# A three-pass graph network: the second edge pass loads edge messages that the first one stored, instead of computing them again

## The chip, the cores and the metric

The kernel runs on one core of one Trainium2 chip. The metric is the device time of one execution in microseconds (us), as the median of three unprofiled runs. The engines are PE (TensorE), DVE (VectorE), ACT (ScalarE), POOL (GpSimd) and SP (SyncE, which here issues DMAs only).

## The reference

The graph has 12,500 nodes of 96 features and 412,500 directed edges, sorted by their target node. Two GINE convolutions are followed by a residual layer norm, and then by a message-passing layer with batch statistics over all edges and nodes:

```python
e = relu(edge_weight @ W_l0 + b_l0) @ W_l1 + b_l1      # (edges, 96), the same e in both convolutions
def gine_conv(x, W1, b1, W2, b2):
    msg = relu(x[src] + e)
    h = x + segment_sum(msg, dst)
    return relu(relu(h @ W1 + b1) @ W2 + b2)
h = relu(gine_conv(relu(gine_conv(x, ...)), ...))
x = layernorm(x + h)
# then: edge_feat = mlp(edge_attr_4), message = mlp([x[src], x[dst], edge_feat]),
# out = layernorm(x + segment_sum(message, dst) + mlp(x)); each mlp normalizes over all its rows
```

## The kernel before

**Work.** Edges are cut into 124 slabs of 26 tiles of 128 edges. A slab is worked on in seven chunks: six of four tiles and one of two. Three passes go over all 868 chunks: `conv0` (first convolution), `conv1` (second convolution, and beside it the edge features of the last layer and their batch statistics, `stats=True`) and `last`. A loop iteration `k` covers four slabs, `Q = 28` chunks, so a pass has 31 iterations. Chunk `q` of iteration `k` has the running number `n = Q*k + q`.

**One chunk of a convolution.** POOL gathers the source nodes' rows with one indirect DMA for each tile (`gather`, L264), 104 for an iteration and 3,224 for a pass, 9,672 in all. PE makes the hidden edge layer (`hidden`, L543, bank `ps_hid`), ACT applies its relu (`relu_hidden`, L556), PE makes the edge message (`pre`, L1309) in one of two banks `ps_pre`. DVE adds the gathered rows in the bank (`add_gathered`, L641). The result is split into three bf16 parts so that a bf16 matmul sums it exactly: ACT takes part one (L582), DVE subtracts it (L589), ACT takes part two (`second_part`, L595), DVE part three (`third_part`, L600). DVE also makes a one-hot matrix of the targets (L1385), and PE sums the chunk into a window of nodes (`segment`, L606, bank `ps_win`). In `conv1` PE also makes the edge features (L549), ACT applies their relu (L562) and DVE takes their statistics (L628).

**Order.** Each engine has its own instruction stream. `staged` writes it: a plan is a list of (lag, stage), and in step `q` every stage does its work for chunk `q - lag`. Semaphores count chunks. A stage waits for the count of what it reads, and for the count that says its buffer is free. `pre` of chunk n waits for part three of chunk n-2, since there are two banks. Node layers of finished nodes are placed beside the chunks from iteration 8 on.

**POOL's waits.** The gathers of chunk n wait until the rows of chunk n-28 have been added (`add`), since the row buffers hold an iteration. Two more waits in `close` tie POOL to PE:

```python
if i == 0:
    sem, count = "seg", Q * k + q - 4 - (6 if opening(k) else 0)
elif i == 2:
    sem, count = "pre", Q * k + q - 1 - (4 if opening(k) else 0)
```

The first gather of a chunk waits until `segment` is four chunks behind at most, the third until `pre` is one behind. In `conv0` these two waits begin with iteration `NEAR = 3`; in the other passes they are there from the start.

Of the kernel before, what the change touches and what calls it, by code (L numbers as in the profile page):

```python
# [18 lines left out]
F32 = mybir.dt.float32  # L19
# [18 lines left out]
Q = V * NC_  # L38
QH = U * NC_
# [68 lines left out]
def staged(eng, iters, width, plan, ahead=None, start=None, side=()):  # L108

    parts = V // U
    half = width // parts

    def beside(k, late, q):
        h, at = q // half, q % half
        for place, stage in side:
            if late > 0 and place == at:
                stage((k - start) * parts + h)
            if (late > 1 or (late and h)) and place == at + half:  # L120
                stage((k - start) * parts + h - 1)
# [12 lines left out]
    for place, stage in side:  # L134
        if place >= half and start < iters:
            stage((iters - start) * parts - 1)
    for q in range(max(lag for lag, _ in plan)):
        for lag, stage in plan:
            if q < lag:
                stage(iters - 1, width + q - lag)  # L140
# [8 lines left out]
def gnn_kernel(nc, a, out):  # L149
# [22 lines left out]
    with ctx:  # L172
# [70 lines left out]
        w_hid0_rows = nc.dram_tensor("w_hid0_rows", (KW, C), BF16, kind="Internal").ap()  # L243
        near = nc.dram_tensor("near", (S, T * P), BF16, kind="Internal").ap()
# [164 lines left out]
        def edge_pass(name, table, y=None, split_edges=False, stats=False, last=False):  # L409
# [8 lines left out]
            with ExitStack() as st:  # L418
# [18 lines left out]
                hid = [sb(f"{name}_hid{i}", [P, CH * P], F32, st) for i in range(2)]  # L437
# [35 lines left out]
                if not last:  # L473
                    z = sb(f"{name}_z", [C1, STEP], F32, st)
                    END = STEPS - inner_steps(N, NPAD, S)
                    assert END % 2 == 0 and 2 * STEP <= 512
# [25 lines left out]
                turned = [x[:, 512 - W:512] for x in ps["win"]]  # L502
                s = Sems(st, name)
# [4 lines left out]
                NEAR = 3  # L508

# [8 lines left out]
                def load_rows(sp, r, slab):  # L518
# [3 lines left out]
                    for i in range(3):  # L522
                        sp.dma_start(row[r][AT + i * n:AT + (i + 1) * n, :], src[:, at]).then_inc(s[f"row{r}"], 16)
# [22 lines left out]
                def features(pe, r, q, b, n, free):  # L546
                    t0, nt = CHUNKS[q % NC_]
                    need(pe, s["rf"], n)
                    pe.matmul(ps["feat"][0][0:C, 0:nt * P], w_hid1[0:KE, 0:C], srow[r][:, t0 * P:(t0 + nt) * P],  # L549
                              start=True, stop=True).then_inc(s["f"], 1)  # L550
# [7 lines left out]
                def relu_features(act, q, b, n, free):  # L558
                    nt = CHUNKS[q % NC_][1]
                    act.wait_ge(s["f"], n + 1)  # L560
                    need(act, s["bn"], free)
                    act.activation(feat[b][:, 0:nt * P], ps["feat"][0][0:C, 0:nt * P], ACT.Relu).then_inc(s["rf"], 1)  # L562
# [74 lines left out]
                def add_gathered(v, j, q, b, n):  # L637
                    t0, nt = CHUNKS[q % NC_]
                    v.wait_ge(s["pre"], n + 1)
# [325 lines left out]
                def tensor_end(pe):  # L965
                    for r in range(U):
                        pe.wait_ge(s[f"win{r}"], ITERS * PAIRS)
                    pe.wait_ge(s["step"], STEPS - END + 1)
                    for w in ENDS:
# [38 lines left out]
                def scalar_end(act):  # L1008
# [3 lines left out]
                    if split_edges:  # L1012
# [3 lines left out]
                        for w in ENDS:  # L1016
                            act.activation(sums[0:C, end_at(w):end_at(w) + 2 * STEP], one[w][0:C, :], ACT.Relu,
                                           bias=b_conv[l][1][:]).then_inc(s["e_sums"], 1)
                        return
# [130 lines left out]
                def sync_windows(sp):  # L1150
# [29 lines left out]
                    def slab_rows(k, j):  # L1180
                        r = j % U
                        free("hid", k, j)
                        if stats:
                            free("f", k, j)
                        load_rows(sp, r, k * V + j)
# [67 lines left out]
                def gpsimd_windows(gp):  # L1253
                    def close(k, q, i):
# [4 lines left out]
                        elif i == 2:  # L1259
# [28 lines left out]
                def tensor_windows(pe):  # L1288
                    def hidden_rows(k, q):
                        j, c, _, _ = chunk(q)  # L1290
                        r = j % U
                        if c == 0:
                            pe.wait_ge(s[f"row{r}"], ROWS * (turn(k, j) + 1))
                        hidden(pe, r, q, Q * k + q)
                        if stats:
                            if c == 0:
                                pe.wait_ge(s[f"srow{r}"], 48 * (turn(k, j) + 1))
                            features(pe, r, q, q % 2, Q * k + q, left(k, q))

# [34 lines left out]
                    staged(pe, ITERS, Q, [(0, hidden_rows), (1, pre), (4, turn_window), (3, segment)],  # L1334
                           start=START, side=([] if last else [(4, summed)]) + node_stages(pe))

                def scalar_windows(act):
                    plan = [(0, lambda k, q: relu_hidden(act, q, q % 2, Q * k + q, left(k, q)))]
                    if stats:
                        plan += [(0, lambda k, q: relu_features(act, q, q % 2, Q * k + q, left(k, q)))]  # L1340
# [4 lines left out]
                    plan += [(2, lambda k, q: second_part(act, q, q % 2, Q * k + q)), (1, message)]  # L1345
                    if last:
                        plan += [(1, lambda k, q: square_message(act, q, q % 2, Q * k + q, left(k, q)))]
                    staged(act, ITERS, Q, plan, ahead=(lambda k: copy_piece(act, k)) if split_edges else None,
                           start=START, side=node_stages(act))

                def vector_windows(v):
# [38 lines left out]
                    def add_rows(k, q):  # L1390
# [5 lines left out]
                        add_gathered(v, j, q, q % 2, Q * k + q)  # L1396
# [110 lines left out]
                def vector_general(v):  # L1507
# [3 lines left out]
                    def body(k):  # L1511
# [6 lines left out]
                        for c, (t0, nt) in enumerate(CHUNKS):  # L1518
# [17 lines left out]
                            add_gathered(v, 0, c, 0, n)  # L1536
# [390 lines left out]
```

## Time and profile before

| What | Value |
|---|---|
| Median of three unprofiled runs | 12209.71 us (12207.5 to 12210.12) |
| Span of the profiled execution | 14691.4 us |
| PE busy in that span | 9543.3 us, 65% |
| DVE busy | 7533.7 us, 51% |
| ACT busy | 4925.7 us, 34% |
| POOL busy | 9148.4 us, 62% |
| DMA | 647.55 MB, mean 44 GB/s |

The profiled execution's own time is its span, from the first to the last instruction of the program. It is 20% longer than the unprofiled median. Busy shares are over the whole span; the three passes take about a third of it each (`conv0` to 4,859 us, `conv1` from 4,880 to 9,729 us, `last` from 9,770 us), and a short stretch of final layers ends it. Times of POOL's gathers are those of writing the descriptors; the data moves afterwards.

### The profile page before, as it was taken

Reading aid. Unit: us, or ns where it says so; the run is one execution under the profiler, and the core shown is the slowest. Engines: PE = TensorE matmul, PEld = TensorE weight load, DVE = VectorE, ACT = ScalarE, POOL = GpSimd, SP = SyncE. Lnnn points to the kernel's source line nnn. Section 1 sums busy time; section 2 is a strip of 40 time slices with the busy share of each in tenths; the row PEclk is TensorE's granted clock in tenths of the full one; section 3 lists DMA queues with packets and bytes.
Section 4 is the critical chain, followed back from the end, with each engine's and each line's share of the span. In section 5 each row is a group of like instructions: output and inputs, shape, how many; then the busy total and the mean of one; then the engine's idle time right before and its main releaser. Section 6 shows DMA issues by size and latency. Waiting matters only on the chain. (4 is left out here: it accounts for less than half of the span.)

```text
span 14691.4 us, 164775 instructions
## 1 busy us (share of the span) xinstructions
PE 9543.3 (65%) x34164; PEld 6790.2 (46%) x34164; DVE 7533.7 (51%) x15604; ACT 4925.7 (34%) x11020; POOL 9148.4 (62%) x9725
## 2 busy tenths in 40 slices
PE   3666666666666677777777777766555555555556
PEld 2544444444444444455555555544444444444444
DVE  3433434334333444455555555556666666666666
ACT  2322222222222333333333333333333333333333
POOL 6466666666666566666666666656666666666665
PEclk9999999999999655555555555555555555555555
DMA  3111111111111211122222222211122222212122
GB/s 80 32 40 40 40 41 40 41 40 40 41 40 40 54 42 43 43 47 45 46 46 46 47 46 45 47 43 41 42 45 43 44 43 44 44 44 44 43 44 47
DMA packets 580837, 647.55 MB, mean 44 GB/s; under 512 B 411208, under 2 KB 411689, under 8 KB 579722
## 3 DMA queue, kind: packets, MB, share of 16 engines
q0 software_dynamic: 309504, 476.02, 15.5%
q1 hardware_dynamic: 219142, 139.69, 3.9%
q10 hardware_dynamic: 51712, 27.54, 0.7%
q14 instruction: 432, 3.54, 0.1%
q8 instruction: 47, 0.77, 0.0%
HBM read 604.68 MB, written 39.43 MB: 44 GB/s over the span
## 5 line engine op out<-in xcount | busy, mean ns | idle before, releaser
L1309 PE MATMUL ps_pre<-w_e,conv_hid 97*128 97x96 f32 x12896 | 3268.4, 433 | 2144.1 <-DVE conv_part L600 1554.4
L1309 PEld LDWEIGHTS ps_pre<-w_e,conv_hid 97*128 97x128 f32 x12896 | 2873.9, 326 | 2886.6 <-issue 2393.8
L1309 PE MATMUL ps_pre<-last_w_q,last_hid 128*128 128x96 f32 x6448 | 1627.8, 432 | 1540.8 <-issue 935.3
L1309 PEld LDWEIGHTS ps_pre<-last_w_q,last_hid 128*128 128x128 f32 x6448 | 1440.1, 327 | 1928.3 <-issue 1605.6
L264 POOL DMA_INDIRECT early_got<-in_x_rows,early_idx x1612 | 1524.3, 946 | 960.5 <-issue 439.0
L264 POOL DMA_INDIRECT early_got<-h_rows,early_idx x1612 | 1520.8, 943 | 944.2 <-issue 478.3
L264 POOL DMA_INDIRECT early_got<-p_rows,early_idx x1612 | 1520.4, 943 | 926.6 <-issue 463.3
L264 POOL DMA_INDIRECT last_got<-p_rows,early_idx x1612 | 1520.8, 943 | 905.0 <-issue 430.5
L264 POOL DMA_INDIRECT conv_got<-h_rows,early_idx x1612 | 1520.8, 943 | 884.0 <-issue 435.6
L264 POOL DMA_INDIRECT conv_got<-in_x_rows,early_idx x1612 | 1520.7, 943 | 853.1 <-issue 447.1
L582 ACT ACTIVATE conv_part<-ps_pre 128x384 bf16<-128x384 f32 x1736 | 816.0, 470 | 3676.9 <-DVE ps_pre L641 2405.4
L606 PE MATMUL ps_win<-conv_part,conv_hot 128*112 128x288 bf16 x6448 | 1904.0, 445 | 0.6 <-DVE conv_part L600 0.5
L556 ACT ACTIVATE conv_hid<-ps_hid 96x512 f32<-96x512 f32 x1736 | 972.8, 560 | 2311.5 <-remote 1488.0
L641 DVE TENSOR_TENSOR ps_pre<-ps_pre,early_got 128x384 f32<-128x384 f32 x1302 | 697.2, 536 | 1982.9 <-remote 697.7
L1385 DVE TENSOR_TENSOR conv_hot<-ps_own,rel 128x448 bf16<-128x448 f32 x1736 | 1016.2, 585 | 1082.3 <-remote 359.4
L543 PE MATMUL ps_hid<-conv_row,w_hid 12*96 12x512 bf16 x1736 | 1084.7, 625 | 545.4 <-issue 343.6
L606 PEld LDWEIGHTS ps_win<-conv_part,conv_hot 128*112 128x112 bf16 x6448 | 1290.7, 214 | 78.0 <-DVE conv_part L600 2.5
L641 DVE TENSOR_TENSOR ps_pre<-ps_pre,conv_got 128x384 f32<-128x384 f32 x868 | 466.5, 537 | 1469.3 <-remote 715.4
L628 DVE BATCH_NORM_STATS2 conv_parts<-conv_feat 96x6 f32<-96x512 f32 x868 | 563.8, 649 | 782.4 <-issue 460.0
L606 PE MATMUL ps_win<-last_part,last_hot 128*112 128x291 bf16 x3224 | 964.0, 450 | 0.6 <-DVE last_part L600 0.5
L595 ACT CAST conv_part<-ps_pre 128x384 bf16<-128x384 f32 x1736 | 787.7, 454 | 469.8 <-DVE ps_pre L589 269.7
L600 DVE TENSOR_TENSOR conv_part<-ps_pre,conv_part 128x384 bf16<-128x384 f32 x1736 | 905.0, 521 | 77.7 <-issue 65.4
(255 smaller groups left out, 10572.7 us busy)
## 6 DMA issues: line engine op xcount, KB each, us to landing
conv_row<-ea_parts SPq DMA_DIRECT2D x372, 84.5 KB
last_row<-ea_parts SPq DMA_DIRECT2D x372, 84.5 KB
early_got<-in_x_rows,early_idx POOLq DMA_INDIRECT x1612
conv_got<-in_x_rows,early_idx POOLq DMA_INDIRECT x1612
early_got<-h_rows,early_idx POOLq DMA_INDIRECT x1612
conv_got<-h_rows,early_idx POOLq DMA_INDIRECT x1612
early_got<-p_rows,early_idx POOLq DMA_INDIRECT x1612
last_got<-p_rows,early_idx POOLq DMA_INDIRECT x1612
```

The lines of the kernel that those rows point to most:

```text
L264: gp.indirect_dma_start(to[:, t * C:(t + 1) * C], None, table, bass.IndirectOffsetOnAxis(index[:, t:t + 1], 0)).then_inc(sem, 16)
L543: pe.matmul(ps["hid"][0][0:HC, 0:nt * P], w_hid[:], row[r][AT:AT + K, t0 * P:(t0 + nt) * P], start=True, stop=True).then_inc(s["hid"], 1)
L556: act.activation(hid[b][0:C, 0:nt * P], ps["hid"][0][0:C, 0:nt * P], ACT.Relu).then_inc(s["rhid"], 1)
L582: act.activation(part_of(q, 0, nt)[:, :, 0:C], m3, ACT.Relu).then_inc(s["part0"], 1)
L595: act.copy(part_of(q, 1, nt)[:, :, 0:C], tiles_of(ps["pre"][b], nt, C)).then_inc(s["part1"], 1)
L600: v.tensor_tensor(part_of(q, 2, nt)[:, :, 0:C], tiles_of(ps["pre"][b], nt, C), part_of(q, 1, nt)[:, :, 0:C], ALU.subtract).then_inc(s["par ...
L606: return pe.matmul(bank[0:W, 0:3 * M].rearrange("p (i c) -> p i c", i=3), hot_b[:, t * W:(t + 1) * W], parts, start=start, stop=stop)
L628: v.bn_stats(parts[:, c * 6:(c + 1) * 6], feat[b][:, 0:nt * P]).then_inc(s["bn"], 1)
L641: v.tensor_tensor(at, at, got[j][:, t0 * C:(t0 + nt) * C], ALU.add).then_inc(s["add"], 1)
L1309: mm = pe.matmul(ps["pre"][q % 2][:, t * C:(t + 1) * C], hid[q % 2][0:P if last else C1, t * P:(t + 1) * P], w_q[j % U][:, c * C:(c + 1) * ...
L1385: v.tensor_tensor(hot[q % 2][:, 0:nt * W].rearrange("p (t w) -> p t w", w=W), iota[:, 0:W].unsqueeze(1).to_broadcast([P, nt, W]), rel[:, b ...
```

## The change

`e` is the same in both convolutions, so `conv0` keeps it. There ACT copies the message from the PSUM bank to one of four SBUF ring buffers before the rows are added (`keep_messages`), and one step later issues a DMA that stores the chunk in a DRAM tensor `e_rows` (`store_messages`, 128 partitions of 1,536 bytes for a four-tile chunk, 192 KB). DVE's `add_gathered` waits for the copy (`ecp`) in place of PE's `pre`.

In `conv1` the hidden layer and `pre` are gone from PE, `relu_hidden` from ACT, the loads of the edge weights from SP and the wait on `pre` from POOL. ACT issues a load of the chunk three of its steps ahead (`load_messages`) and copies it into the bank (`bring_messages`). ACT's plan is shifted by two steps against the others for that, and the edge features get a second PSUM bank.

```diff
-                for i in range(3):
+                for i in range(3 if weights else 0):
...
+                def keep_messages(act, k, q, b, n):
+                    nt, slot = CHUNKS[q % NC_][1], q % ER
+                    act.wait_ge(s["pre"], n + 1)
+                    need(act, s[f"est{slot}"], 16 * (USES * k + q // ER))
+                    act.copy(e_ring[slot][:, 0:nt * C], ps["pre"][b][:, 0:nt * C]).then_inc(s["ecp"], 1)
...
+                def store_messages(act, k, q, n):
+                    j, _, t0, nt = chunk(q)
+                    slot = q % ER
+                    act.wait_ge(s["ecp"], n + 1)
+                    act.nop(nofuse=True)
+                    act.dma_start(e_rows[bass.ds(k * V + j, 1), :, t0 * C:(t0 + nt) * C].rearrange("s p c -> (s p) c"),
+                                  e_ring[slot][:, 0:nt * C]).then_inc(s[f"est{slot}"], 16)
...
+                def load_messages(act, k, q, n):
+                    need(act, s["ecp"], n + 1 - ER)
+                    act.dma_start(e_ring[slot][:, 0:nt * C], e_rows[...]).then_inc(s[f"eld{slot}"], 16)
+                def bring_messages(act, k, q, b, n, free):
+                    act.wait_ge(s[f"eld{slot}"], 16 * (USES * k + q // ER + 1))
+                    need(act, s["part2"], free)
+                    act.copy(ps["pre"][b][:, 0:nt * C], e_ring[slot][:, 0:nt * C]).then_inc(s["ecp"], 1)
...
-                    v.wait_ge(s["pre"], n + 1)
+                    v.wait_ge(ready, n + 1)
...
-                        elif i == 2:
+                        elif i == 2 and not stats:
...
-                    staged(pe, ITERS, Q, [(0, hidden_rows), (1, pre), (4, turn_window), (3, segment)],
+                    staged(pe, ITERS, Q, [(0, hidden_rows), *([] if stats else [(1, pre)]), (4, turn_window), (3, segment)],
...
+                    elif stats:
+                        plan = [(0, lambda k, q: load_messages(act, k, q, Q * k + q)),
+                                (SHIFT + 1, lambda k, q: bring_messages(act, k, q, q % 2, Q * k + q, left(k, q))),
+                                (SHIFT, lambda k, q: relu_features(act, q, q % 2, Q * k + q, left(k, q))),
+                                (SHIFT + 2, second), (SHIFT + 1, message)]
+                    else:
+                        plan = [(0, hidden_part), (2, second),
+                                (1, lambda k, q: keep_messages(act, k, q, q % 2, Q * k + q)), (1, message),
+                                (2, lambda k, q: store_messages(act, k, q, Q * k + q))]
```

Line numbers in the rows below this point are each kernel's own. ACT in the middle of `conv0`, two steps before:

```order
L556 ACTIVATE conv0_hid1<-ps1_hid0 96x512
L595 CAST conv0_part3<-ps1_pre1 128x4x96
L582 ACTIVATE conv0_part0<-ps1_pre0 128x4x96
L554 REGISTER_ALU
L556 ACTIVATE conv0_hid0<-ps1_hid0 96x512
L595 CAST conv0_part0<-ps1_pre0 128x4x96
L582 ACTIVATE conv0_part1<-ps1_pre1 128x4x96
```

ACT at the same place now (L570 is `relu_hidden`, L642 `second_part`, L583 the new copy, L629 part one, L591 the store with the empty instruction ahead of it):

```order
L570 ACTIVATE conv0_hid1<-ps1_hid0 96x512
L642 CAST conv0_part1<-ps1_pre1 128x4x96
L583 COPY conv0_e_ring2<-ps1_pre0 128x384
L629 ACTIVATE conv0_part2<-ps1_pre0 128x4x96
L591 ISA
L591 DMA e_rows<-conv0_e_ring1 128x384
L568 REGISTER_ALU
L570 ACTIVATE conv0_hid0<-ps1_hid0 96x512
L642 CAST conv0_part2<-ps1_pre0 128x4x96
L583 COPY conv0_e_ring3<-ps1_pre1 128x384
L629 ACTIVATE conv0_part3<-ps1_pre1 128x4x96
```

Each step has gained a copy between part two of one chunk and part one of the next, and a store at its end.

PE in the middle of `conv1` before (L543 hidden layer, L549 features, L1309 `pre`, L606 `segment`):

```order
L543 MATMUL ps2_hid0<-conv1_row1,w_hid0_64 96x512
L549 MATMUL ps2_feat0<-conv1_row1,w_hid1 96x512
L1309 MATMUL ps2_pre0<-w_e0,conv1_hid0 128x96 x4
L606 MATMUL ps2_win1<-conv1_part2,conv1_hot0 112x288 x4
L543 MATMUL ps2_hid0<-conv1_row1,w_hid0_64 96x512
```

PE there now (L563 is the features' matmul, L653 `segment`):

```order
L563 MATMUL ps2_hid0<-conv1_row1,w_hid1 96x512
L653 MATMUL ps2_win1<-conv1_part2,conv1_hot0 112x288 x4
L563 MATMUL ps2_feat0<-conv1_row1,w_hid1 96x512
L653 MATMUL ps2_win1<-conv1_part3,conv1_hot1 112x288 x4
L563 MATMUL ps2_hid0<-conv1_row1,w_hid1 96x256
```

The hidden layer and the four `pre` matmuls of a chunk are gone, and the features alternate between two banks.

ACT in the middle of `conv1` now (L600 load, L609 copy into the bank, L576 relu of the features); before, the step held L556, L562, L595 and L582:

```order
L600 ISA
L600 DMA conv1_e_all<-e_rows 128x384
L609 COPY ps2_pre0<-conv1_e_all 128x384
L574 REGISTER_ALU
L576 ACTIVATE conv1_feat1<-ps2_hid0 96x512
L642 CAST conv1_part1<-ps2_pre1 128x4x96
L629 ACTIVATE conv1_part2<-ps2_pre0 128x4x96
```

One activation has gone and one copy has come, and the load is issued at the head of the step.

## Rows read from the trace of the kernel before

**Rows 1.** The page's head: span, busy time of each engine and instructions.

```profile
span 14691.4 us, 164775 instructions
PE 9543.3 (65%) x34164; PEld 6790.2 (46%) x34164; DVE 7533.7 (51%) x15604; ACT 4925.7 (34%) x11020; POOL 9148.4 (62%) x9725
```

**Rows 2.** Timeline of POOL around conv0's end: start, duration, idle before and its releaser.

```profile
4836.65 0.94 POOL L264 DMA_INDIRECT conv_got<-in_x_rows,early_idx  x1 [2.87 <-remote]
...
4850.38 0.95 POOL L264 DMA_INDIRECT conv_got<-in_x_rows,early_idx  x1 [0.30 <-issue]
4854.37 0.94 POOL L264 DMA_INDIRECT conv_got<-in_x_rows,early_idx  x1 [3.04 <-remote]
...
4858.11 0.94 POOL L264 DMA_INDIRECT conv_got<-in_x_rows,early_idx  x1 [0.30 <-issue]
4879.71 0.94 POOL L264 DMA_INDIRECT early_got<-h_rows,early_idx  x1 [20.65 <-issue]
```

**Rows 3.** Timeline of POOL: first gather, end of conv1, start of last, last gather.

```profile
2.76 1.14 POOL L264 DMA_INDIRECT early_got<-in_x_rows,early_idx  x1 [2.33 <-DMA early_idx<-in_src_t]
...
9727.86 0.94 POOL L264 DMA_INDIRECT conv_got<-h_rows,early_idx  x1 [0.30 <-issue]
...
9770.50 0.95 POOL L264 DMA_INDIRECT early_got<-p_rows,early_idx  x1 [23.62 <-issue]
...
14618.69 0.95 POOL L264 DMA_INDIRECT last_got<-p_rows,early_idx  x1 [0.30 <-issue]
```

**Rows 4.** Gathers (L264), conv1 and last: window, length, busy (count), clock, DMA share, GB/s.

```profile
5000.00:9700.00 4700.00, 2944.48 (x3122) 0.50 0.20 45
9800.00:14600.00 4800.00, 3007.23 (x3189) 0.50 0.20 43
```

**Rows 5.** Timeline of POOL in conv0, around the start of iteration 3.

```profile
458.34 0.94 POOL L264 DMA_INDIRECT conv_got<-in_x_rows,early_idx  x1 [0.30 <-issue]
547.10 0.94 POOL L264 DMA_INDIRECT early_got<-in_x_rows,early_idx  x1 [87.81 <-PE ps_win L606]
```

**Rows 6.** Windows there: PE, PEld, DVE, ACT, POOL busy, clock, DMA; then L641 alone.

```profile
461.30:558.70 97.40, 91.45 (x340) 68.24 (x341) 60.70 (x125) 41.47 (x85) 7.78 (x9) 1.00 0.06 13
461.30:558.70 97.40, 15.07 (x28) 1.00 0.06 13
```

**Rows 7.** Timeline of all engines in that stretch, one chunk of conv0.

```profile
485.84 2.02 PE L1309 MATMUL ps_pre<-w_e,conv_hid 97*128 97x96 f32 x8
486.60 0.48 ACT L595 CAST conv_part<-ps_pre 128x384 bf16<-128x384 f32 x1
487.90 0.57 DVE L641 TENSOR_TENSOR ps_pre<-ps_pre,early_got 128x384 f32<-128x384 f32 x1 [1.33 <-PE ps_pre L1309]
488.38 0.55 DVE L600 TENSOR_TENSOR conv_part<-ps_pre,conv_part 128x384 bf16<-128x384 f32 x1
488.50 0.49 ACT L582 ACTIVATE conv_part<-ps_pre 128x384 bf16<-128x384 f32 x1 [1.42 <-DVE ps_pre L641]
489.07 0.50 PE L1309 MATMUL ps_pre<-w_e,conv_hid 97*128 97x96 f32 x1
```

**Rows 8.** Timeline: conv0's first add of gathered rows.

```profile
120.93 0.57 DVE L641 TENSOR_TENSOR ps_pre<-ps_pre,early_got 128x384 f32<-128x384 f32 x1 [1.30 <-PE ps_pre L1309]
```

**Rows 9.** DMAs: an issue by ACT (timeline); two 192 KB stores with their landing.

```profile
7007.28 0.38 ACTq L776 DMA_DIRECT2D nf_rows<-nf  x1
h_rows<-conv_got SPq DMA_DIRECT2D x2, 192.0 KB, 2.2
```

**Rows 10.** The two largest waits of POOL on PE in conv1: us, times, longest.

```profile
POOL early_got L264 <- PE ps_pre L1309: 95.2, 55, 3.1
POOL early_got L264 <- PE ps_win L606: 60.2, 28, 19.1
```

**Rows 11.** Timeline of the first microseconds: a gather and a DVE cast.

```profile
15.97 1.99 POOL L264 DMA_INDIRECT early_got<-in_x_rows,early_idx  x1 [0.30 <-issue]
15.98 1.85 DVE L363 CAST rel<-dst_i 128x3224 f32<-128x3224 int32 x1 [3.64 <-DMA dst_i<-in_dst_t]
```

More of the change, by code:

```diff
@@ L38 @@
 Q = V * NC_
+ER = 4
+USES = Q // ER
 QH = U * NC_
@@ L133, in staged @@
     phases(eng, iters, iters if start is None else start, body)
[L134 to L137, printed above, removed]
+    rest = [(place - half, stage) for place, stage in side if place >= half and start < iters]
+    for q in range(max([lag for lag, _ in plan] + [place + 1 for place, _ in rest])):
+        for place, stage in rest:
+            if place == q:
+                stage((iters - start) * parts - 1)
         for lag, stage in plan:
@@ L436, in edge_pass @@
                 row = [sb(f"{name}_row{r}", [AT + K, T * P], BF16, st) for r in range(U)]
-                hid = [sb(f"{name}_hid{i}", [P, CH * P], F32, st) for i in range(2)]
+                if last:
+                    e_ring = None
+                elif stats:
+                    e_all = sb(f"{name}_e_all", [P, ER * CH * C], F32, st)
+                    e_ring = [e_all[:, i * CH * C:(i + 1) * CH * C] for i in range(ER)]
+                else:
+                    e_ring = [sb(f"{name}_e_ring{i}", [P, CH * C], F32, st) for i in range(ER)]
+                hid = ([e_all[:, i * CH * P:(i + 1) * CH * P] for i in range(2)] if stats else
+                       [sb(f"{name}_hid{i}", [P, CH * P], F32, st) for i in range(2)])
                 msg = [sb(f"{name}_msg{i}", [P, CH * C], F32, st) for i in range(2)] if last else None
@@ L502, in edge_pass @@
                 turned = [x[:, 512 - W:512] for x in ps["win"]]
+                feat_banks = [ps["feat"][0], ps["hid"][0]] if stats else None
                 s = Sems(st, name)
@@ L508, in edge_pass @@
                 NEAR = 3
+                SHIFT = 2
                 def left(k, q):
@@ L547, in features @@
                     t0, nt = CHUNKS[q % NC_]
-                    need(pe, s["rf"], n)
-                    pe.matmul(ps["feat"][0][0:C, 0:nt * P], w_hid1[0:KE, 0:C], srow[r][:, t0 * P:(t0 + nt) * P],
+                    need(pe, s["rf"], free)
+                    pe.matmul(feat_banks[b][0:C, 0:nt * P], w_hid1[0:KE, 0:C], srow[r][:, t0 * P:(t0 + nt) * P],
                               start=True, stop=True).then_inc(s["f"], 1)
@@ L1018, in scalar_end @@
                                            bias=b_conv[l][1][:]).then_inc(s["e_sums"], 1)
+                        for slot in range(ER):
+                            act.wait_ge(s[f"est{slot}"], 16 * USES * ITERS)
                         return
@@ L1181, in slab_rows @@
                         r = j % U
[L1182 to L1185, printed above, removed]
+                        free("f" if stats else "hid", k, j)
+                        load_rows(sp, r, k * V + j, weights=not stats)
                         if last:
@@ L1292, in hidden_rows @@
                         if c == 0:
-                            pe.wait_ge(s[f"row{r}"], ROWS * (turn(k, j) + 1))
-                        hidden(pe, r, q, Q * k + q)
+                            pe.wait_ge(s[f"srow{r}" if stats else f"row{r}"], (48 if stats else ROWS) * (turn(k, j) + 1))
                         if stats:
-                            if c == 0:
-                                pe.wait_ge(s[f"srow{r}"], 48 * (turn(k, j) + 1))
                             features(pe, r, q, q % 2, Q * k + q, left(k, q))
+                        else:
+                            hidden(pe, r, q, Q * k + q)
                     def pre(k, q):
@@ L1395, in add_rows @@
                                 v.wait_ge(s[f"got{j}{g}"], 16 * (t1 - t0) * (k + 1))
-                        add_gathered(v, j, q, q % 2, Q * k + q)
+                        add_gathered(v, j, q, q % 2, Q * k + q, s["pre" if last else "ecp"])
                     def add_constants(k, q):
@@ L1535, in body @@
                                 v.wait_ge(s["qadd"], 2 * n + 2)
-                            add_gathered(v, 0, c, 0, n)
+                            add_gathered(v, 0, c, 0, n, s["pre"])
                             subtract_first(v, c, 0, n)
```

31 lines of the change are left out of this document (21 added, 10 removed).

## The prediction

> **What bounds the kernel now.** I read the page's head first [rows 1]: PE 65%, POOL 62%, DVE 51%, ACT 34%. No engine is full, so the head doesn't name the bound. The timeline of POOL does. Between two waits, twelve gathers of `conv0` start from 4836.65 to 4850.38 us [rows 2], that is 13.73 / 11 = 1.248 us from one start to the next, of which 0.94 is the gather and 0.30 the issue of the next. Multiply it out: 9,672 gathers x 1.248 = 12,070.7 us. Outside that train lie the start, 2.76; the turn from `conv0` to `conv1`, 4879.71 - 4858.11 - 1.25 = 20.4 [rows 2]; the turn to `last`, 9770.50 - 9727.86 - 1.25 = 41.4; and what follows the last gather's slot, 14691.4 - 14618.69 - 1.25 = 71.5 [rows 3]. Together 136.0, the sum 12,206.7. The unprofiled median is 12,209.7. So the unprofiled kernel is POOL issuing gathers without a stop, with 3 us left for real waits; the rounding of the two rows (0.001 us a gather) makes that 3 +- 10. If a slot were only the mean gather, 2944.48 / 3122 = 0.943 [rows 4], and 0.30, the sum would be 12,158 and waits could hold at most 51 us.
>
> The profiled execution lasted 14,691.4 us [rows 1], 2,485 us more than this sum. POOL's timeline shows where: waits of some 3 us put down to "remote", one 4850.38 to 4854.37, the last 4836.65 [rows 2], about 18 us apart, that nothing in the program ends. Both later passes pay the same for them, 4700 / 3122 = 1.505 and 4800 / 3189 = 1.505 us a gather [rows 4], though their layers on the other engines differ. I take them for an effect of the recording. They are not in the median, so my sum is made against the 12,206.7, that is the profiled time without them, which stands 0.02% below the median; differences go on the median as they are. The profiled span after the change can't be compared with 14,691.4 to better than these waits repeat.
>
> The consequence: work taken from PE, ACT or DVE is worth only as much as POOL waits for it, and work added costs only as much as it makes POOL wait.
>
> **The one place where POOL waits for real: `conv0`, iteration 3.** POOL runs three iterations ahead without a bond to PE, and the first gather of iteration 3 waits until `segment` is at chunk 80. In the profile that is 87.81 us, ended by PE [rows 5]. Unprofiled, POOL is there at 2.76 + 312 x 1.248 = 392.1 us. The first add is at 120.93 [rows 8]. In this stretch, with POOL out of the way, 28 chunks took 97.40 us, or 3.48 each, with PE busy for 91.45 of them, 94% [rows 6]. So chunk 80 is summed at 120.9 + 81 x 3.48 + 1.2 for its `segment` = 404.0, and POOL waits 12 us, at the edge of the 3 +- 10 that the sum leaves. From there POOL needs 4.99 us for a four-tile chunk and PE 3.48, and the wait doesn't come back.
>
> **What `conv0` gains in work.** ACT's copy, priced by the cast of the same 128x384 from the bank, 0.48 [rows 7], plus a hand-over between engines: part one starts 0.03 after the add's end (488.50 - 487.90 - 0.57), so 0.52. It lies between `pre` and the add. Follow the loop: `pre` begins at 485.84, the add at 487.90 (2.06), DVE's third part of the chunk before at 488.38 (0.48), and that frees the bank for the `pre` of the next chunk at 489.07 (0.69) [rows 7]. The loop is 3.23, under the 3.48 that PE needs. With the copy it is 3.75, and DVE's order, add before third part, keeps it in a line. PE's chunk of 3.48 is no longer the longer one: +0.27 a chunk. Up to chunk 80 that is 81 x 0.27 = **+22 us**, and POOL's wait grows from 12 to 34. Whether ACT is free when `pre` ends: part two ends at 486.60 + 0.48 = 487.08, 0.8 before [rows 7]. The store's issue, 0.38 [rows 9], and an empty instruction stand behind part one, so the next relu starts about 0.3 late and the margin is still 0.5. Bounds: nothing, if the compute is over 34 us earlier at chunk 80 than I have it; and with nothing hidden, 0.52 + 0.43 for the store, 0.95 x 81 = +77. In the rest of the pass the loop of 3.75 stays under POOL's 4.99, 1.2 us to spare a chunk, and costs nothing; if POOL were not the bound there it would be +0.27 x 787 = +212, but the sum above excludes it. The ring has four buffers: a store has two steps, 7 us at the least, to land, and a store of 192 KB landed in 2.2 us [rows 9]. Nothing.
>
> **What `conv1` loses and gains.** On PE the hidden matmul and the eight `pre` instructions of a chunk, 2.02 us [rows 7], go. ACT trades an activation for a copy and an issue, about equal. POOL's waits on PE there are the largest candidates, 95.2 us in 55 waits of at most 3.1, and 60.2 in 28 waits with one of 19.1 [rows 10]. Waits of 3.1 at most are as long as the recording's own, and the sum of the median has no room for 155 us. I take 0, between 0 and -13 (the 3 + 10). The load is issued three ACT steps ahead, at least 11 us against a landing of 2.2, hidden. At the pass's start the first load and copy take the place of the hidden layer and `pre`; the first gathers land in the meantime. The two ends of the pass I put at +-1.
>
> **Transfers.** 868 chunks, 158.5 MB, are stored in one pass and loaded in the next, in 4,024 us of unprofiled pass 39 GB/s, over the 45 that flow now at a DMA share of 0.20 [rows 4]. A doubled share leaves the engines 60% idle, and POOL waits for a gather's descriptors, never for its landing, since an add has an iteration of slack. The gathers' own duration decides: 0.943 in `conv1` and in `last` alike [rows 4], whatever else flows. It was longer in one place only, 1.99 us beside DVE's cast of 128x3224 in SBUF, 15.97 against 15.98 us [rows 11]. The copies added here are ACT's. By the Trainium skill, "DMA: Bandwidth & Descriptors", SWDGE vs HWDGE vs iDMA, GpSimd writes its descriptors to rings in SBUF, a DVE in its two-port mode locks it out of there, and DMAs issued by ACT or SP are immune to that; by that rule the added transfers cost POOL nothing, and the trace agrees where it has anything to show, the long gather beside the cast.
>
> Sum: 0 at the start, +22 at iteration 3, 0 in the steady state, 0 in `conv1`, 0 in `last`: 12,209.7 + 22 = **12,232 us**.
>
> **Rivals.** *A. Nothing measurable* (24%): the change works, PE's load in `conv1` falls, and the compute of the opening is early enough, or ACT's copy hidden well enough, that POOL's wait at iteration 3 hardly grows. For it: the 3 us that the sum leaves are less than my wait of 12. Against: the wait's releaser is PE in the trace, and the loop has no slack. 12,195 to 12,220.
>
> *B. Faster* (12%): the slot is 1.243 and not 1.248, waits hold 51 us, and 12 of them are iteration 3's. The other 39 then sit in POOL's waits on `pre` and `segment` in `conv1` [rows 10] and vanish with the work: 12,209.7 - 39 + 0 to 10 = 12,171 to 12,185. Against it: over eleven gathers in a row the slot is 1.248, and ACT's chain in `conv1` isn't shorter.
>
> *C. Clearly slower* (18%): the added transfers lengthen the gathers themselves. A tenth of a microsecond on one gather of each of the 1,736 chunks of the two convolutions is +174: 12,383; a gather in fifty at 1.99 in place of 0.94, 129 x 1.05, +135. It passes my forecast's upper side from 0.03 us a chunk on. The mildest form, or a store issue that falls ahead of the copy in the opening, ends at 12,260 to 12,300. Against: the constant 0.943. The Trainium skill, in the section Issuing engines are not separate DMA queues of the same page, says that all DMAs run on the same 16 engines and interleave. By that rule gathers would land later. The rows can show a share of 0.20 only, and no run here shows one of 0.4 yet.
>
> **How the numbers follow.** A measurement of this kernel can tell about 0.2%, 24.4 us, from no change: below 12,185.3 or above 12,234.1. My forecast, a growth of POOL's wait by 10 to 50 us (12,215 to 12,260), has 46%; its point lies so near the bound that I split it 25 within, 21 above. A's 24% are all within. Of B's 12%, 11 are faster. Of C's 18%, all slower. That gives 0.11, 0.50, 0.39. The range of 12,180 to 12,300 leaves out the faster half of B and all of C but its mild form, near 2 in 10; the forecast's own is 12,215 to 12,260.
>
> **What the profile after would show.** Right: L641's adds in the stretch where POOL waits at iteration 3 some 3.75 us apart in place of 3.48, and that wait longer; gathers still 0.943; no wait of POOL on `pre` in `conv1`; PE's busy time at least 1,600 us less (868 chunks at 2.02, one in seven of them half as long); the same gaps at the turns; 317 MB more traffic. Wrong: adds still 3.48 apart (A), gathers longer than 0.943 (C), or gathers closer than 1.248 in a row (B). A turn from `conv0` to `conv1` longer than 20.4 by over 5 us would be something I haven't priced, as would a wait of POOL on `add` in steady `conv0`.

## The result and the profile after

The changed kernel takes **12,293.7 us** (median of 4 runs, 12,288.8 to 12,295.6) against 12,209.9 before (4 runs, 12,207.5 to 12,211.4): ratio 1.0068, 95% interval 1.0054 to 1.0083. It is slower by 84 us. My range of 12,180 to 12,300 holds it, at its very end; it lies outside the 12,215 to 12,260 of the forecast itself, whose point, 12,232, had a quarter of the loss.

The page's head of the changed kernel:

```profile
span 12291.5 us, 156248 instructions
PE 7643.8 (62%) x26848; PEld 5238.2 (43%) x26848; DVE 7456.9 (61%) x15604; ACT 5238.6 (43%) x11888; POOL 9156.0 (74%) x9725
```

The span is 2 us under the unprofiled median. The waits of 3 us that fill the trace of before [rows 2] are gone, and this was not the change's doing: a second trace of the kernel before, taken with the first experiments, is free of them too. It is the one to compare with:

```profile
span 12212.2 us, 164775 instructions
PE 9514.6 (78%) x34164; PEld 6795.0 (56%) x34164; DVE 7482.9 (61%) x15604; ACT 4878.6 (40%) x11020; POOL 9153.9 (75%) x9725
```

The spans differ by 79.3 us. PE has lost 1,871 us of work, ACT has gained 360, and POOL's own time is the same. Where the 79 us lie is read from POOL. The start of iteration 3, in the changed kernel:

```profile
396.51 0.94 POOL L268 DMA_INDIRECT conv_got<-in_x_rows,early_idx  x1 [0.30 <-issue]
427.05 0.94 POOL L268 DMA_INDIRECT early_got<-in_x_rows,early_idx  x1 [29.59 <-PE ps_win L653]
```

and in the second trace of before:

```profile
396.64 0.94 POOL L264 DMA_INDIRECT conv_got<-in_x_rows,early_idx  x1 [0.30 <-issue]
398.46 0.94 POOL L264 DMA_INDIRECT early_got<-in_x_rows,early_idx  x1 [0.88 <-PE ps_win L606]
```

POOL arrives at the same moment in both and now waits 29 us longer. That is the wait of [rows 5]. A second one follows six gathers on. The waits of POOL from 440 to 4,000 us (us in all, times, longest), changed kernel first:

```profile
POOL early_got L268 <- PE ps_pre L1357: 75.4, 81, 5.4
POOL conv_got L268 <- PE ps_pre L1357: 34.1, 112, 0.3
```

and before:

```profile
POOL conv_got L264 <- PE ps_pre L1309: 29.3, 96, 0.3
POOL early_got L264 <- PE ps_pre L1309: 23.5, 77, 0.3
```

A wait of 0.3 is only the issue of the next gather, named after the semaphore that it reads. Longer ones exist in the changed kernel alone, and all of them are at one place: gather 6 of an iteration, the third of its chunk 1, which waits for `pre`. I worked the following out from the gathers' start times, less 1.249 us each:

| Waits of POOL in `conv0`, us | before | after |
|---|---|---|
| opening, before iteration 3 | 5.4 | 5.4 |
| iteration 3, its first gather | 0.6 | 29.3 |
| iteration 3, gather 6 | 1.4 | 5.1 |
| gather 6 of iterations 4 to 30 | 0.0 | 45.5 (25 waits of 1.6 to 2.1) |

The difference is 78.0 of the 79.3. `conv1` and `last` are nearly alike: from first to last gather 4,027.1 and 4,025.4 us after, 4,024.2 and 4,025.3 before.

**What gather 6 waits for.** ACT at the start of iteration 18 (timeline, changed kernel):

```profile
2400.98 0.49 ACT L629 ACTIVATE conv_part<-ps_pre 128x384 bf16<-128x384 f32 x1 [1.90 <-DVE ps_pre L688]
2401.15 0.34 ACTq L591 DMA_DIRECT2D e_rows<-conv_e_ring  x1
2404.79 0.51 ACT L1286 COPY ps_e<-conv_e_f 128x416 f32<-128x416 f32 x1 [3.32 <-issue]
```

The last instruction of iteration 17 is the store's issue; the first of iteration 18 is the copy of a piece of edge attributes. Between them ACT stands, for nothing that the profile names ("issue"). DVE waits behind it, then has five instructions on that piece, and only then its third part:

```profile
2405.43 0.59 DVE L1295 CAST conv_e_p<-ps_e 128x416 bf16<-128x416 f32 x1 [4.48 <-ACT ps_e L1286]
...
2408.45 0.55 DVE L647 TENSOR_TENSOR conv_part<-ps_pre,conv_part 128x384 bf16<-128x384 f32 x1
```

PE's `pre` of chunk 27 needs that bank, and POOL that `pre`:

```profile
2409.05 0.74 PE L1357 MATMUL ps_pre<-w_e,conv_hid 97*128 97x96 f32 x2 [8.94 <-DVE conv_part L647]
2411.00 0.94 POOL L268 DMA_INDIRECT early_got<-in_x_rows,early_idx  x1 [2.31 <-PE ps_pre L1357]
```

At the same place before, ACT goes on at once and DVE waits 1.12:

```profile
2346.78 0.49 ACT L582 ACTIVATE conv_part<-ps_pre 128x384 bf16<-128x384 f32 x1 [3.01 <-DVE ps_pre L641]
2347.24 0.51 ACT L1237 COPY ps_e<-conv_e_f 128x416 f32<-128x416 f32 x1
2347.87 0.59 DVE L1246 CAST conv_e_p<-ps_e 128x416 bf16<-128x416 f32 x1 [1.12 <-ACT ps_e L1237]
```

The record of ACT's sequencer, which the timeline leaves out, says what ACT does in the gap (start, duration, operation; after, then before):

```
2401.59 0.04 L93 COMPARE_BRANCH        2346.85 0.04 L91 COMPARE_BRANCH
2404.65 0.05 L93 FUSED_REGOPS          2347.09 0.05 L91 FUSED_REGOPS
```

It is the branch back to the loop's first instruction. I call the time from the branch's end to that instruction the turn: 2.9 us in the median of 21 after, 0.19 before. An iteration of that loop holds 365 of ACT's instructions after and 197 before. So two theories stood against each other: the loop's turn (theory 1), and the copy that now lies between `pre` and the add (theory 2). A third is the traffic of the stores (theory 3).

### The profile page after: what moved, and what is told of

The parts are those of the page before. It is cut to its first block and busy times, and to the rows that moved or that the text cites. A ratio compares the mean times of both kernels' runs of the same rounds, so it can differ in the third digit from the quotient of the medians.

```text
span 12291.5 us, 156248 instructions
## 1 busy us (share of the span) xinstructions
PE 7643.8 (62%) x26848; PEld 5238.2 (43%) x26848; DVE 7456.9 (61%) x15604; ACT 5238.6 (43%) x11888; POOL 9156.0 (74%) x9725
## 5 line engine op out<-in xcount | busy, mean ns | idle before, releaser
L653 PE MATMUL ps_win<-conv_part,conv_hot 128*112 128x288 bf16 x6448 | 1937.9, 451 | 1811.8 <-DVE conv_part L647 1811.6
L1357 PE MATMUL ps_pre<-w_e,conv_hid 97*128 97x96 f32 x6448 | 1630.6, 433 | 937.8 <-DVE conv_part L647 928.2
L653 PEld LDWEIGHTS ps_win<-conv_part,conv_hot 128*112 128x112 bf16 x6448 | 1207.0, 209 | 2234.7 <-DVE conv_part L647 2140.3
L629 ACT ACTIVATE conv_part<-ps_pre 128x384 bf16<-128x384 f32 x1736 | 815.8, 470 | 2800.7 <-DVE ps_pre L688 2763.8
L1357 PEld LDWEIGHTS ps_pre<-w_e,conv_hid 97*128 97x128 f32 x6448 | 1440.7, 328 | 1318.8 <-issue 1041.7
L653 PE MATMUL ps_win<-last_part,last_hot 128*112 128x291 bf16 x3224 | 964.4, 450 | 1.2 <-DVE last_part L647 1.1
L642 ACT CAST last_part<-ps_pre 128x384 bf16<-128x384 f32 x868 | 397.9, 458 | 1310.7 <-DVE ps_pre L636 1308.5
L642 ACT CAST conv_part<-ps_pre 128x384 bf16<-128x384 f32 x1736 | 785.7, 453 | 342.4 <-DVE ps_pre L636 327.8
L636 DVE SCALAR_TENSOR_TENSOR ps_pre<-ps_pre,conv_part 128x384 f32<-128x384 f32 x1736 | 912.4, 526 | 0.1
```

Source lines behind the costliest of these rows:

```text
L629: act.activation(part_of(q, 0, nt)[:, :, 0:C], m3, ACT.Relu).then_inc(s["part0"], 1)
L636: v.scalar_tensor_tensor(out=m3, in0=m3, scalar=0.0, in1=part_of(q, 0, nt)[:, :, 0:C], op0=ALU.max, op1=ALU.subtract).then_inc(s["rem"], 1)
L642: act.copy(part_of(q, 1, nt)[:, :, 0:C], tiles_of(ps["pre"][b], nt, C)).then_inc(s["part1"], 1)
L653: return pe.matmul(bank[0:W, 0:3 * M].rearrange("p (i c) -> p i c", i=3), hot_b[:, t * W:(t + 1) * W], parts, start=start, stop=stop)
L1357: mm = pe.matmul(ps["pre"][q % 2][:, t * C:(t + 1) * C], hid[q % 2][0:P if last else C1, t * P:(t + 1) * P], w_q[j % U][:, c * C:(c + 1) * ...
```

## The experiments

The times of before were taken in each job; the jobs of one group share them.

**A second trace of before** (no edit).

> The kernel before, unchanged, for a second trace. Theory 1 (ACT's loop turn): the trace of the change shows ACT standing 2.8 us at every turn of its conv0 loop, between the branch and the next instruction, and POOL waiting 1.6 to 2.1 us at the third gather of chunk 1 of 26 iterations, 50.6 us in all. In the kernel before ACT's turn should take 0.2 us again, that gather should wait under 0.3 us, and the wait at iteration 3 should be under 5 us, so that conv0's waits sum to some 85 us less than after. Theory 2 (the copy alone): the turn takes about as long as after the change and the third gather waits between 0 and 1.5 us, less by the 0.5 of the copy. If the waits of 3 us every 18 us appear again, the trace leaves this open.

Measured: one run of 12,214.0, and the rows above: turn 0.19, no wait at gather 6 after iteration 3, and 78 us less of waits in `conv0`, where I had expected 85. That is what theory 1 expects. The trace also refutes what I took for an effect of the recording: it is a recording too, and has none of the 3 us waits.

**`conv0` of the change with `conv1` of before.**

Against before, with the two functions and DVE's wait on `ecp` as in the change:

```diff
-                    plan += [(2, lambda k, q: second_part(act, q, q % 2, Q * k + q)), (1, message)]
+                    plan += [(2, lambda k, q: second_part(act, q, q % 2, Q * k + q))]
+                    if split_edges:
+                        plan += [(1, lambda k, q: keep_messages(act, k, q, q % 2, Q * k + q))]
+                    plan += [(1, message)]
+                    if split_edges:
+                        plan += [(2, lambda k, q: store_messages(act, k, q, Q * k + q))]
```

> conv0 of the change (copy, stores) with conv1 of before, which computes its messages itself and reads nothing back. Everything lost in conv0: 12,294 us, within 5 us of the change. If conv1's loads or its lighter engines had a part in it, the time moves away from that: loads that cost something would make this one faster than the change by their price, a gain in conv1 would make it slower.

Measured: 12,290.4 (12,286.3 to 12,291.5), ratio 1.0065 (1.0048 to 1.0082), before 12,210.8. All but 3 to 4 us is lost in `conv0`; `conv1`'s loads, its idle PE and its changed ACT are together worth no more than that, and in the traces the pass `conv1` is longer by 2.8 us with them.

**The copy without the stores.**

Against the kernel of the experiment above (the copy's wait for the ring's store goes too):

```diff
-                    if split_edges:
-                        plan += [(2, lambda k, q: store_messages(act, k, q, Q * k + q))]
```

> conv0 with ACT's copy of the messages to the ring, but no stores of them; conv1 as before. ACT's conv0 loop holds 227 instructions in place of 365. Theory 1 (ACT's loop turn, which grows with what the loop holds): the turn takes 0.2 us, the wait at the third gather of chunk 1 all but vanishes, the growth at iteration 3 stays in part (81 chunks at 3.7): 12,230 us, between 12,220 and 12,240. Theory 2 (the copy between pre and add does it all): 12,290 us. Theory 3 (the traffic of the stores): 12,210 us.

Measured: 12,238.4 (12,236.8 to 12,240.5), ratio 1.0022 (1.0013 to 1.0032). The turn is 0.20 with 225 instructions in the loop, and gather 6 waits only in iteration 3 (2.1). POOL at that iteration's first gather (its timeline):

```profile
421.62 0.94 POOL L267 DMA_INDIRECT early_got<-in_x_rows,early_idx  x1 [25.01 <-PE ps_win L625]
```

So the copy alone costs 24.8 us at iteration 3 (24.7 + 2.1 against 2.0) and nothing later. Theory 2 falls as an explanation of the rest. Theory 3 falls only as an explanation of the whole: this run takes away the stores' traffic together with their instructions, so it can't tell whether the other 52 us are due to the traffic or to the longer loop. The next runs can.

**96 empty instructions that did not come to be.** The plain empty instructions were left out when the program was built, so this run repeats the changed kernel: its trace has as many of ACT's instructions ahead of the loop as that one's.

> The change with 96 empty instructions on ACT ahead of conv0's loops, which run once, during the opening, and move every later instruction of ACT by 96 places. Theory 1, in the form that the turn is slow where the loop lies badly against the blocks in which instructions are fetched: the turn in at least one of conv0's two loops, and perhaps in conv1's, changes from 2.8 to 0.2 us or the other way, and POOL's 1.9 us an iteration with it: 12,235 us if both change, 12,294 if neither does. If the number of instructions in the loop alone decides: 12,294 and a turn of 2.8 us everywhere. Theory 2 (the copy): 12,294.

Measured: 12,294.7 (12,291.0 to 12,297.5), turns of 2.8 and 2.9 in `conv0`. It says nothing on the theories.

**ACT's loops moved by 96 places, and by 32.**

```diff
+                    if split_edges:
+                        for _ in range(96):      # 32 in the other
+                            act.wait_ge(s["set_fits"], 1)
+                            act.nop(nofuse=True)
                     staged(act, ITERS, Q, plan, ahead=(lambda k: copy_piece(act, k)) if split_edges else None,
```

> The change with 96 empty instructions, each behind a wait that is long satisfied so that they do stand in the program, on ACT ahead of conv0's loops; they run once, during the opening. The loops' contents are the same 343 and 365 instructions, 96 places further on. From the turns seen so far I fit this: instructions are held in blocks of 128, three of them reach back, and with an offset of 120 a loop of ACT turns slowly if it touches a fourth block. By that fit both loops of conv0 turn in 0.2 us at this place: POOL's waits at the third gather of chunk 1 vanish (about 50 us), the wait at iteration 3 falls by 3 to 10, 12,238 us, between 12,230 and 12,245. If the length of the loop alone decides: turns of 2.8 us and 12,293 as after the change. If the copy or the stores' issue make the wait: 12,293 too.

> The same with 32 instructions in place of 96, the control of the run above. By the fit both loops of conv0 still touch a fourth block: turns of 2.8 us and 12,293 us. If the added instructions help by anything else than the place they give the loop, this one is faster than the change as well.

In this job the kernel before took 14,696.4 us (12 runs). Moved by 96: 14,730.5, ratio 1.0023 (1.0013 to 1.0033). Moved by 32: 14,795.6, ratio 1.0059 (1.0042 to 1.0076). The turns of `conv0` came out as the fit in these expectations says: 0.19 and 0.20 us (the loop to iteration 7, and the one from 9) against 2.90 and 2.76. The same loops, with the same contents, are worth 65 us between two places. The first was run again:

> The same kernel as shift96, once more: in that job the kernel before itself took 14,696 us and not 12,210, so the difference is wanted where it takes 12,210. Theory 1: turns of 0.2 us in conv0, no wait at the third gather of chunk 1, and of the 84 us some 55 back: 12,238 us. If the kernel before takes 14,700 again: 30 to 40 us above it.

Measured: 12,259.4 (8 runs, 12,242.8 to 12,261.2), before 12,225.4 (12,223.2 to 12,228.3): ratio 1.0028 (1.0017 to 1.0038), 34 us above before, as in the other job, where I had expected 28. Its profiled execution, the one of 12,242.8 (the other seven took 12,258.7 to 12,261.2), spans 12,241.0, which is 28.8 above the second trace of before. ACT at the start of iteration 18 there, and POOL at iteration 3:

```profile
2374.51 0.34 ACTq L591 DMA_DIRECT2D e_rows<-conv_e_ring  x1
2375.34 0.51 ACT L1286 COPY ps_e<-conv_e_f 128x416 f32<-128x416 f32 x1 [0.52 <-issue]
...
424.67 0.94 POOL L268 DMA_INDIRECT early_got<-in_x_rows,early_idx  x1 [27.60 <-PE ps_win L653]
```

Stores, copy and traffic are all there, and gather 6 waits in no iteration after 3. Theory 3 falls with it. In iteration 3 POOL waits 27.3 us at the first gather and 2.6 at gather 6, which is 3.1 more than with the copy alone; that much belongs to the stores or to the 96 added pairs, and I can't tell which.

**The loop made long in the kernel before.**

```diff
+                    def empty(k, q):
+                        for _ in range(6):
+                            act.wait_ge(s["set_fits"], 1)
+                            act.nop(nofuse=True)
+                    if split_edges:
+                        plan += [(2, empty)]
```

with eight more such pairs ahead of the loops, for their place.

> The kernel before with six empty instructions a step in ACT's conv0 loops (each behind a wait that is long satisfied), which makes these loops as long as the change's, 343 and 365, and nothing else: no copy, no store, no transfer. By the fit both touch a fourth block of 128. Theory 1: the turn takes 2.8 us; without the copy's 0.5 in the chain the third gather of chunk 1 waits 1.0 to 1.6 us an iteration, 25 to 45 in all, and the wait at iteration 3 is 5 to 10: 12,250 us, between 12,235 and 12,265. If the stores or the copy are needed for a slow turn: 0.2 us and 12,210.

Measured: 12,279.8 (12,277.9 to 12,280.9), ratio 1.0044 (1.0027 to 1.0061), 54 us above before; I had said 12,235 to 12,265 where before takes 12,210, which is 25 to 55 above it, so this is the upper end. The turns are 2.36 and 2.98. ACT and POOL at an iteration's start:

```profile
2378.53 0.51 ACT L1237 COPY ps_e<-conv_e_f 128x416 f32<-128x416 f32 x1 [3.38 <-issue]
...
2384.74 0.95 POOL L264 DMA_INDIRECT early_got<-in_x_rows,early_idx  x1 [2.31 <-PE ps_pre L1309]
```

Gather 6 waits 46.9 us after iteration 3 (expected 25 to 45), as much as in the changed kernel, without a copy or a store; at iteration 3 there are 4.0 more. The six instructions a step may add a little to that themselves; I can't tell it apart.

**POOL's waits on PE taken out.** Without the one on `pre`, and without both:

```diff
-                        elif i == 2 and not stats:
+                        elif i == 2 and last:
```
```diff
-                        body(k, near=True)
+                        body(k, near=not split_edges)
```

> The change with POOL's wait on pre, ahead of the third gather of a chunk, taken out of conv0 too (the waits on segment and on the rows' buffers stay). ACT's loop still turns in 2.8 us, but POOL no longer waits for pre behind it: the 50 us of the steady iterations and the 5 at iteration 3's second chunk go, the 29 at its start stay: 12,240 us, between 12,232 and 12,250. If the wait on segment takes over at the next gather, it stays above 12,270.

> The change without either of POOL's two waits on PE in conv0; the gathers wait only until their buffer is free, 28 chunks back. ACT's turn of 2.8 us and the chunk of 3.7 us stay, but POOL's 4.99 us for a four-tile chunk absorbs both: 12,210 us, within 5 us of the kernel before. If these waits hold something together that the gathers need, for instance if gathers become longer than 0.943 us when POOL runs further ahead, it is slower by that.

Measured, with before at 14,696.4: 14,857.7, ratio 1.0099 (1.0082 to 1.0116), and 14,925.3, ratio 1.0160 (1.0143 to 1.0177). Both expectations missed: they are 161 and 229 us above before, where I had expected 30 and 0. Against `shift32`, which in the same job has the slow turns and both waits, taking out the waits costs 62 and 130 us. Again, where before took 12,225.4:

> The same kernel as no_pre_wait, once more. Where the kernel before takes 12,210: 12,240, since POOL no longer stands behind pre and there is no other wait late enough. If the 160 us that it lost against before in the last job come from the missing wait itself and not from the state of that job, it is slower than the change here too, above 12,294.

> The same kernel as no_near_waits, once more. In the last job it lost 229 us: POOL ended conv0 early and the turn to conv1 took 121 us in place of 28, since the adds were behind. Where the kernel before takes 12,210, a chunk of conv0 takes 3.7 us of compute against 4.99 of gathers, the adds catch up after some hundred chunks, and the turn stays at 21: 12,210 us, within 5 us. If running ahead costs by itself: above 12,240.

Measured: 12,268.4 (12,255.6 to 12,270.8), ratio 1.0035 (1.0023 to 1.0048), and 12,229.1 (12,226.7 to 12,232.6), ratio 1.0003 (0.9994 to 1.0013). With ACT turning in 2.9 us and the copy in the chain, the changed kernel is as fast as before once POOL doesn't wait for PE, as expected. Without the `pre` wait alone it is 43 us above before, where I had expected 30: iteration 3's start stays (27.0), and the wait on `segment` takes over a part, 4.1 us at gather 8 of iteration 3 and some 0.5 in many later ones. POOL from 440 to 4,000 us:

```profile
POOL early_got L268 <- PE ps_win L653: 38.9, 96, 4.4
```

Most of these 96 are the 0.3 of an issue. No version beat the kernel before, nor could one by this road: outside the turns between the passes, POOL waits only 7 us in the second trace of before.

## Why the prediction was right in the range and short in the sum

- **What bounds the kernel** held. The gathers stand 1.249 to 1.252 us apart in every trace but those of the job of 14,696 us (I had 1.248). In the second trace of before the ends outside them sum to 127.7 us, where I had 136.0, and the waits to 7.4, where I had 3: two small errors that nearly cancel. Rival B, that 39 us of waits sit in `conv1`, is out: they were 0. Rival A, nothing measurable, is out by the 84 us.
- **The profiled time.** I took the 3 us waits for an effect of the recording. That was wrong: a whole job ran at 14,696 us unprofiled, and its traces have the same waits. My sum without them still came within 6 us of the undisturbed span of 12,212.2.
- **Iteration 3** was the right place, and its term the right size for what it covered: +22 forecast, 24.8 by the copy alone. The adds there, 26 in each window (length, busy), changed kernel and second trace of before:

```profile
330.30:422.20 91.90, 13.41 (x26) 1.00 0.33 88
```
```profile
308.60:393.30 84.70, 13.41 (x26) 1.00 0.23 48
```

Over 25 steps from add to add that is 3.67 against 3.38, +0.29 where I had +0.27. The timeline shows two four-tile chunks in a row 3.71 apart (forecast 3.75), and ACT's copy as the add's releaser:

```profile
400.43 0.57 DVE L688 TENSOR_TENSOR ps_pre<-ps_pre,conv_got 128x384 f32<-128x384 f32 x1 [1.69 <-ACT conv_e_ring L583]
404.14 0.57 DVE L688 TENSOR_TENSOR ps_pre<-ps_pre,conv_got 128x384 f32<-128x384 f32 x1 [1.69 <-ACT conv_e_ring L583]
```

Chunk 80 released POOL at 427.05, forecast 425.9, but that closeness is luck. Before, the release was at 398.5 and not at 404: the first add stands at 117.7 in an undisturbed trace and at 120.93 in [rows 8], and a chunk took 3.44 where I had 3.48. POOL itself came at 397.9 and not at 392.1, since I had left out 5.4 us of waits in the opening. So the wait that I put at 12 was 0.6, and it grew by 28.7 and not by 22.
- **The steady state of `conv0`** is the step that failed, at a price of 45.5 us where the sum has 0: "In the rest of the pass the loop of 3.75 stays under POOL's 4.99 ... and costs nothing." The average has that room and the turn of an iteration hasn't. There DVE stands behind ACT's copy of a piece and has five instructions of its own, so the slack of POOL's third gather is used up. I never looked at a turn. The changed kernel lost 45.5 us at gather 6 after iteration 3, and `shift96_b` and `before_long` show that it is ACT's slow turn: taken away it is 0, put into the kernel before it is 46.9. The same turns delay chunk 80 and gather 6 of iteration 3 by 4.5 us in all (34.4 in the changed kernel against 29.9 in `shift96_b`).
- **The range** holds the result by luck. Its part above 12,260 was there for rival C's mildest form, longer gathers or a store's issue ahead of the copy. Neither happened; a turn of ACT's loop was in none of my terms.
- **Transfers** held but for 3 us, and rival C is out at the sizes that it names. All gathers of POOL in most of `conv0` (window, length, busy and count, clock, DMA share, GB/s), changed kernel:

```profile
436.00:4100.00 3664.00, 2732.21 (x2896) 1.00 0.34 86
```

That is 0.943 us a gather, with the DMA share at 0.34 and 86 GB/s where the second trace of before has 0.23 and 48 in its window above. In all, 308 MB more are moved (955.7 against 647.6); I had said 317. The loads have a trace of an effect: a gather of `conv1` takes 944.7 ns in the mean against 943.9 before and 943.8 in `conv0_half`, which has no loads, and over 3,224 gathers that is most of the 2.9 us by which the pass is longer. One reading of mine was wrong. The gather of 1.99 us [rows 11] isn't the only long one: in the same trace one at 46.09 us takes 2.65, and it too begins beside a cast of DVE in SBUF (L389, 46.03 to 47.93).
- **`conv1`**: nothing gained, as forecast. ACT's loop turns slowly there from iteration 9 on in both kernels (2.5 us); no gather waits for it.

The parts sum: copy 24.8, slow turns 45.5 + 4.5, and 3.1 that go with the stores, together 77.9 of 79.3.

## What to carry to other kernels

Before an edit adds instructions to an engine's loop, count what the loop holds and look at its turn in the trace, at the first instruction after the branch; that idle time reads "issue" and is in no average. Compare the slack of a wait at the worst chunk of an iteration, not a chunk's mean time with another's. And work taken from an engine is worth what the bounding engine waited for it, here nothing.

## What the runs showed of the hardware

**A loop's turn is fast or slow by where its instructions lie.** In seven kernels the medians of ACT's loops are 0.12 to 0.21 us or 2.36 to 2.98, but for the first loop of `conv1` in the job of 14,696 us. It stood between: at 1.29 in `shift32`, and at 1.04 in `shift96`, the kernel that has 2.40 there in the other job. The table has `shift96` from that other job (`shift96_b`). For some of ACT's loops: its first and last instruction counted in ACT's program, their number, and the median turn.

| Kernel, loop | first | last | number | turn, us |
|---|---|---|---|---|
| before, `conv0`, from 9 | 687 | 883 | 197 | 0.19 |
| before, `conv1`, from 9 | 1792 | 2072 | 281 | 2.55 |
| conv0_half, `conv1`, the same loop | 2351 | 2631 | 281 | 0.18 |
| after, `conv0`, to iteration 7 | 456 | 798 | 343 | 2.70 |
| after, `conv0`, from 9 | 1071 | 1435 | 365 | 2.92 |
| after, `conv1`, to iteration 7 | 1933 | 2282 | 350 | 0.19 |
| shift96, `conv0`, from 9 | 1167 | 1531 | 365 | 0.20 |
| shift96, `conv1`, to iteration 7 | 2029 | 2378 | 350 | 2.40 |
| shift32, `conv0`, from 9 | 1103 | 1467 | 365 | 2.76 |

One rule fits all 42 loops of the seven kernels. Cut the count, shifted by 120, into blocks of 128 instructions: a loop that lies in three blocks or fewer turns fast, and one that touches a fourth turns slowly (shifts of 121 to 123 do as well, and the loop at 1.29 is counted as slow). The rule was made from 24 of the loops; the other 18 were run after it, and six of these are `last`'s loops, which turn in 0.12 everywhere. It is a fit to this program's ACT. DVE has a loop of 381 instructions that turns in 0.24 us and one of 358 at 2.7 to 2.8; I didn't move those. A rule by the number alone leaves at least 5 of the 42 wrong. The Trainium skill, "Runtime: NRT & Kernel Launch", Instruction fetch mechanics, says that an engine other than TensorE holds two blocks of 256 instructions, and that a taken branch to a target outside them must fetch it first. A stall at the branch of some loops, which comes and goes as a loop is moved, agrees with that; the section gives no price for it, and here it is 2.4 to 3.0 us. The sizes don't agree: two blocks of 256, wherever they begin, leave at least 6 of the 42 wrong, so here the measurement decides. What the fetch itself does in the gap no record shows.

**The same program took 12,210, 12,225 and 14,696 us in three jobs.** The 15 us between the first two are in the gathers themselves. The profiled executions of `before_long` and `no_near_waits_b` are as slow as the others of that job, and their gathers take 945.3 to 946.3 ns in the mean of a pass; `shift96_b`'s and `no_pre_wait_b`'s profiled ones are 11 to 18 us faster than the others of their kernels, and have 943.5 to 944.7, as the traces of the job of 12,210 have. Over 9,672 gathers 1.6 ns are 15 us.

In the last job, as in the trace of [rows 2], POOL stands for some 2 to 4 us at a time, 12 us apart in the median (26 in `conv1` of the changed kernels), and all the engines stand together: in the trace of [rows 2] there are 376 stretches of over 1.5 us between 600 and 14,000 us in which none starts an instruction, in the second trace of before 3. There the changed kernel without POOL's waits on PE is 1.6% above before, where it is level with it otherwise. POOL's waits in iterations 4 to 30 of `conv0` sum to 885 us against 653 in the trace of [rows 2], and most of them are ended by DVE's adds; the last gather of the pass starts 163 us later. Then POOL, ahead of the adds, stands 120 us at the turn to `conv1`, against 20.

```profile
5142.74 0.95 POOL L268 DMA_INDIRECT early_got<-h_rows,early_idx  x1 [120.51 <-issue]
```

What makes these waits is open.
